# Issuing a transformer kernel's DMA transposes from ScalarE's queue, and its weight conversions three at a time

## The reference, cut to what matters

```python
u = layernorm(x)
q = u @ Wq.T                       # 32 heads of 128
lat = [u @ Wk_down.T, u @ Wv_down.T]   # 512 latent features per token, all 4096 tokens
k = lat_k @ Wk_up.T ; v = lat_v @ Wv_up.T
x = x + layernorm(softmax(causal(q k / sqrt(128))) v @ Wo.T)
u = layernorm(x)
x = x + layernorm(u @ base_W.T + lora(u, top-2 of 28 experts))
```

## Time and profile before

| | us |
|---|---|
| median of 2 runs | 5450.72 (5354.54 and 5546.89) |
| the profiled execution: its own time | 5278.84 |
| its span on the slowest core (core 7) | 5277.7 |
| spans of the 8 cores | 5105.4 to 5277.7 |
| TensorE busy, matmuls | 3030.0 (57%) |
| VectorE busy | 1527.7 (29%) |
| ScalarE busy | 1029.4 (20%) |

### The profile page before, as it was taken

The page is one execution under the profiler, slowest core; times in us unless marked ns, Lnnn a source line. Parts: engine busy times, 40 slices in busy tenths (PEclk is TensorE's granted clock), DMA queues, the critical chain, the costliest instruction groups (busy, mean ns, idle before and its releaser), DMA issues.

```text
span 5277.7 us, 36821 instructions; the slowest of 8 cores (5105.4 to 5277.7 us)
## 1 busy us (share of the span) xinstructions
PE 3030.0 (57%) x13056; PEld 1200.8 (23%) x13056; DVE 1527.7 (29%) x2250; ACT 1029.4 (20%) x977; POOL 121.1 (2%) x230
## 2 busy tenths in 40 slices
PE   1111111211112297989893694597998999893694
PEld 0000000000001043323341242242332333341242
DVE  1101010110101101666404103204666666414103
ACT  1000010100001100545202001103544555202001
POOL 1000000000001000000000000000000000000000
PEclk9555555655556698989996697798999999996697
DMA  9999999989998945000252353643000000252253
GB/s 143 109 102 112 103 107 111 106 119 101 122 113 127 172 152 144 1 1 1 63 170 73 89 171 132 168 152 72 1 1 1 1 1 1 72 171 77 84 171 132
DMA packets 329392, 494.21 MB, mean 94 GB/s; under 512 B 278256, under 2 KB 286704, under 8 KB 287232
## 3 DMA queue, kind: packets, MB, share of 16 engines
q0 software_dynamic: 19648, 197.64, 26.4%
q1 hardware_dynamic: 309568, 294.23, 24.1%
HBM read 604.93 MB, written 121.63 MB: 138 GB/s over the span
## 4 chain that ended last, share of the span: by engine, by line
PE 54%; another core or an unknown queue 18%; DMA 9%; DVE 6%; ACT 4%; SPq 4%; issue 2%; DVEq 1%; POOLq 0%; ACTq 0%; POOL 0%
PE psz L455 7%; PE pss L490 6%; DMA UFMA<-UTM 5%; PE psa L364 4%; PE psa L574 4%; PE psb L743 4%; PE psb L574 4%; PE psa L743 4%; PE psb L364 4%; SPq L218 4%; PE psa L462 4%; PE psb L462 4%; DVE BSTAT L194 3%; PE psa L300 3%
## 5 line engine op out<-in xcount | busy, mean ns | idle before, releaser
L300 PE MATMUL psa<-UFMA,WPa 128*128 128x512 bf16 x512 | 146.9, 458 | 1530.8 <-DMA WPa<-WKVD 873.7
L498 ACT ACTIVATE PTD<-pss 128x1024 bf16<-128x1024 f32 x768 | 740.7, 1021 | 665.5 <-PE pss L490 665.5
L504 DVE TENSOR_TENSOR PTD<-PTD,M 128x2048 bf16<-128x2048 bf16 x384 | 470.6, 1225 | 420.1 <-ACT PTD L498 420.1
L490 PE MATMUL pss<-QFM,KFM 128*128 128x512 bf16 x1536 | 403.7, 380 | 68.5 <-ACT PTD L498 45.7
L311 DVE CAST KCVC<-psa 128x512 bf16<-128x512 f32 x16 | 11.1, 692 | 1453.8 <-PE psa L300 1453.8
L300 PEld LDWEIGHTS psa<-UFMA,WPa 128*128 128x128 bf16 x512 | 56.8, 113 | 1620.4 <-issue 1583.3
L455 PE MATMUL psz<-PTD,E 128*16 128x512 bf16 x1536 | 396.8, 381 | 0.2 <-DVE ACC L477 0.2
L206 ACT ACTIVATE STAT<-STAT 128x1 f32<-128x1 f32 x64 | 12.9, 202 | 1819.6 <-DVEq L204 1430.0
L364 PE MATMUL psa<-UFMA,WPa 128*128 128x512 bf16 x1024 | 230.0, 383 | 168.2 <-DMA WPa<-WQB 167.4
L743 PE MATMUL psa<-QFM,WPa 128*128 128x512 bf16 x1024 | 230.6, 384 | 26.1 <-DMA WPa<-BWBMB 26.1
L574 PE MATMUL psa<-QFM,WPa 128*128 128x512 bf16 x1024 | 230.6, 384 | 2.2 <-DVE QFM L528 2.2
(11 more groups left out here) (116 smaller groups left out, 2398.6 us busy)
## 6 DMA issues: line engine op xcount, KB each, us to landing
BWBMB<-BWBM POOLq DMA_DIRECT2D x32, 1088.0 KB, 66.0
WPa<-BWBMB SPq DMA_DIRECT2D x32, 1088.0 KB, 5.5
WPb<-BWBMB SPq DMA_DIRECT2D x32, 1088.0 KB, 5.7
XA<-X POOLq DMA_DIRECT2D x32, 1024.0 KB, 43.0
WQB<-WQ POOLq DMA_DIRECT2D x32, 1024.0 KB, 56.8
WOB<-WO POOLq DMA_DIRECT2D x32, 1024.0 KB, 63.5
WPa<-WQB SPq DMA_DIRECT2D x32, 1024.0 KB, 5.2
WPb<-WQB SPq DMA_DIRECT2D x32, 1024.0 KB, 5.0
```

Of the source, the lines that this page charges most:

```text
L300: ins = TEN.matmul(PSab[pp][:], WP[wp][:, c * 128:(c + 1) * 128], ubuf[:, c * 512:(c + 1) * 512], start=(c == 0), stop=(c == 31))
L490: ins = TEN.matmul(PSS[:, kt * 512:(kt + 1) * 512], KFM[:, kv4 * 512 + kt * 128: kv4 * 512 + (kt + 1) * 128], QFM[:, h * 512:(h + 1) * 512 ...
L498: ins = SCA.activation(PTD[:, ptp * 2048 + hf2 * 1024: ptp * 2048 + (hf2 + 1) * 1024], PSS[:, hf2 * 1024:(hf2 + 1) * 1024], AF.Exp, scale= ...
L504: pm = vS.inc(VEC.tensor_tensor(PTD[:, ptp * 2048:(ptp + 1) * 2048], PTD[:, ptp * 2048:(ptp + 1) * 2048], M01[:], AL.mult))
```

## The change

Two edits. `tr_u` issues its transpose from ScalarE's queue, with its waits there, in place of SyncE's. And the 12 conversions of a block are issued in threes, after each tile's layernorm in the `t4` loop and with no wait of their own, in place of 12 together behind the matmuls of cg 0. Since POOL has no other instruction in the `t4` loop, in POOL's program the 12 now stand together ahead of `pa_loads(ub + 1)` and behind the weights of cg 3 of the block before. Their number per block and in all is the same.

```diff
     def tr_u(dst, tspan, toff, utile, waits, pb):
-        W(SYN, *waits)
+        W(SCA, *waits)
         ap = dst[:].rearrange("p (c t) -> p c t", c=32, t=tspan)[:, :, toff:toff + 128]
-        return sTU[pb].inc(SYN.dma_start(out=ap, in_=utile, transpose=True), 16)
+        return sTU[pb].inc(SCA.dma_start(out=ap, in_=utile, transpose=True), 16)
@@
             free_xa[pb] = (ap_mark, red_mark)
+            pump_conv(3)
             tr_u(ubuf, 512, t4 * 128, ut,
                  [(sS, ap_mark), (tS, ufma_pa[ub % 2]), (vS, ufma_free_v)], pl)
             utm_free[pl] = sTU[pl].v
@@
             if cg == 3:
                 ufma_pa[ub % 2] = mm_mark
-            if cg == 1:
-                W(GPS, (tS, wp_free[0]))
-                pump_conv(12)
             W(VEC, (tS, mm_mark))
```

## The result

The changed kernel is slower by 1.6%: the ratio of its time to that of the kernel before is 1.0157, with a 95% interval of 1.0079 to 1.0236. This ratio is the mean of five executions after (5295.67, 5299.08, 5299.2, 5345.77 and 5363.13 us) over that of four before (5220.45 to 5257.1 us); with the three short ones of the five alone it would be 1.011. The profiled execution took 5298.11 us. I had forecast no change, 5350 us and a ratio of 0.999.

What follows compares the result with a forecast made beforehand. Stage A was taken to be bound by DMA transfers. The terms 35 - 110 + 53 + 16 gave -6 us on 5278.84, 5273 us in the profile; scaled to runs 5350 us, range 5140 to 5580 us.

Steps and rivals of the forecast that it cites:

- (a): Stage A's load queue: same transfers, reordered; PE's wait for cg 2's weights behind conversions goes, gaining under 114.8 us a block.
- (c): Stage A: a block's first transpose ends only after queue 0 drains, blocking ScalarE's next pass and three loads; 6 us.
- (b): Stage A: the first transpose now starts beside the conversions and slows queue 0 by 4 us a block, +35 us.
- rival 3: Stage A, slower: the first transpose holds back the conversions; at 25% +222 us, about 5575 us in runs; chance 0.30.
- rival 2: Stage A, faster by far: transposes get packet bursts, so queue 0 never empties; 5030 us in runs; chance 0.08.
- (d): Stage A: three loads beside the second transpose take 44 us, the end 13; blocks of 215 us, -110 us over six.
- Rival 1: Stage A, faster: three loads beside one transpose stay at full speed, 18 us; 5165 us in runs; chance 0.22.
- (e): Stage A's ends: first block, last block and the stretch to the Q projection sum to 486 against 433 us, +53.
- (f): Transpose calls outside stage A: ScalarE adds 7 us in each of three, less 5 for a Q weight; +16 us.

Runs made afterwards that it cites:

- e1_threes_on_sp: The changed kernel with its transposes put back on SyncE's queue, conversions still in threes; ratio to the kernel before 0.9782 (0.9725 to 0.9839).
- e6: The kernel of e1_threes_on_sp with only the transposes of the two calls outside stage A on ScalarE's queue; core spans 5121.3 to 5139.4 us.

## Why the prediction was wrong

- **The mechanism, steps (a) to (c), was right.** The wait for W2 went, the wait for transposes took its place, T0's issue held ScalarE for 115.69 us in the block shown, and X3, W0, W1 came behind it. Three windows of queue 0 and queue 10 of the changed kernel, 458:478 with conversions alone, 478:570 with conversions beside T0, and 570:590 mostly with loads, show (b) and (c):

```profile
q0 software_dynamic: 98, 2.13, 96.1%
...
q0 software_dynamic: 468, 10.04, 97.9%
q10 hardware_dynamic: 445, 0.11, 0.8%
...
q0 software_dynamic: 393, 2.91, 97.3%
q10 hardware_dynamic: 393, 0.10, 3.7%
```

  Beside T0 a conversion takes 92 us x 1.05 MB / 10.04 MB = 9.6 us, my 9.3 plus the 4 us a block, and queue 0 moves 109 GB/s, 107 in the 20 us before T0; rival 3, a slowdown of 12%, falls. The packets go one for one beside conversions as beside loads, if the completions of queue 0 are counted: 445 with 468, 393 with 393, and in 64:140 us of block 0, 384 with 384. I had counted data packets only, 24 for the 12 conversions; with completions it is 36 an engine, of 256. T0 could not finish under the conversions either way, and rival 2 falls. The rule of the Trainium skill behind rival 2 (DMA: Bandwidth & Descriptors, Queues, rings and completion order: a packet of 9 to 17 descriptors is drained before an engine changes rows) does not describe these transposes, if each record is a descriptor.
- **(d) was mis-sized, without effect.** From T1's issue to the pass of t2 it took 33 us in the block shown, 27 to 35 in all blocks 1 to 6, not 44. The end took 19 us, not 13, since T2's and T3's issues stand between the passes. Together 52 against 57. Rival 1 wanted 18 us, and falls. One of the six waits behind (d), block 4's 44.53 us, lies below the 46.2 to 62.7 that I gave for all; their mean, 59 with the pass, is right.
- **(e), the sum of stage A, held.** Block 218 us against 215, first cg 0 at 219.93 against 216, the Q projection at 1816 against 226 + 6 x 215 + 175 + 85 + 35 = 1811.
- **(f) was small, and a term beside it stood at nothing.** From the Q projection's start to the end the slowest core took 3481 us, 38 more than before (3443); I had 16. The two gates wait 8 us longer each and the second Q projection 7 to 10, so (f) came to 23 to 26: the 5 us that I gave back for the Q weight did not come. Another 11 us lie in two waits for the V up-projection's weights, one for each `ci`, which I had not touched. The first, before and after:

```profile
2082.41 1.86 PE L407 MATMUL psa<-KCVC,WKUS 128*128 128x512 bf16 x4 [23.58 <-DMA WVUSO<-WVUDO]
...
2069.83 0.59 PE L405 MATMUL psa<-KCVC,WKUS 128*128 128x512 bf16 x1 [29.54 <-DMA WVUSO<-WVUDO]
```

  In e1_threes_on_sp they are 32 and 30 us on the slowest core, so they don't come from ScalarE's queue; their cause was not tested.
- **The step that failed is the one from the sum to the ratio**, 5273 on 5278.84, with its baseline. The profile of the changed kernel says 5298, 0.5% more than my sum, some 5 us in stage A and 21 behind it. The larger part is the baseline: 5278.84 was the slowest core of one execution, and the four that the ratio is taken from have a mean of 5238, 0.8% less. 5273 over 5238 is 1.007, 5298 over 5238 is 1.011, and the two longer executions make it 1.016. Stage A of core 7 ended at 1834 us in my trace; the other seven cores ended theirs at 1679 to 1778. Each of my terms describes cores in step with conversions of 9.3 us. The kernel before had that nearly only on its slowest core, and in most executions not even there: its slowest core ends at 5193 to 5263 there. The views for this were at hand. I read the span of every core in the table and asked nothing of its 172 us.
- In **terms of the experiments**, from the short executions: conversions ahead, cores in step, 5234 to 5102 us, -132 (before to e1; 5234 is the median of before); ScalarE's queue outside stage A about +37 (e1 to e6; one execution of e6); in stage A +158 (e6 to the changed kernel), of which 147 are there when the Q projection starts, some 20 a block. -132 + 37 + 158 = +63. My (c) had that +158 as a mechanism and never priced what the change would be without it; the sentence by which the move to ScalarE would be 0 and the sum 16 us lower counted (f) alone, where the move costs 195.
- The scale of 5350 us was a guess between two runs; the five executions compared lie at 5296 to 5363. That 5350 lies inside this range is luck.

## What to carry to other kernels

Before moving a DMA issue to another engine's queue, find the longest time that this issue took on the old one, and list what stands behind it on the new engine and whom that releases; here one 4.4 us pass released three loads, and putting the issue behind the pass recovered about two thirds of the loss in stage A (104 of 158 us). And where a kernel's cores share memory, read the span of each core before the sum is made: here a spread of 3% among cores with the same program meant that a stage had two speeds, and a change of order cost all of them the faster one.

## What the runs showed of the hardware

- Two cores of a pair converting side by side wrote 111 GB/s each, and one whose partner didn't convert up to 200 GB/s; in the trace of the kernel before, how many of the other six cores converted made no more than 6 GB/s of difference. With a third of the bytes taken away 1 MB took 6.0 us in place of 9.3.
- A transpose issued beside a full queue of another engine does not slow that queue (97.9% of the engines' time with T0 in flight, 96.1% without), but it gets one 256-byte packet for each packet of that queue, large or small, and its issue blocks the issuing engine up to 141 us.
- A transpose that starts first and then meets loads goes with a slow stretch of both: 66 us for four loads in place of 24. ScalarE's wait in it varied from 22 to 75 us under the same two loads. Why, stays open.
